# Filling the key and value buffers on ScalarE and adding the gathered rows in the transfer

## What is computed

```python
def _edge_attention(xn, edge_index, ef, ew, Wq, bq, Wk, bk, Wv, bv, We, be, Wo, bo):
    q = (xn @ Wq + bq).reshape(n, H, DH)          # H = 8 heads of DH = 32
    k = (xn @ Wk + bk).reshape(n, H, DH)
    v = (xn @ Wv + bv).reshape(n, H, DH)
    ep = ef @ We + be                             # the edge part, 32 numbers for all heads
    scores = jnp.einsum('ehd,ehd->eh', q[dst], k[src] + ep[:, None, :]) * scale
    scores = scores * ew[:, None]
    m = jax.ops.segment_max(scores, dst, num_segments=n)
    ex = jnp.exp(scores - m[dst])
    s = jax.ops.segment_sum(ex, dst, num_segments=n)
    attn = ex / s[dst]
    out = jax.ops.segment_sum(attn[:, :, None] * v[src], dst, num_segments=n)
    return out.reshape(n, D) @ Wo + bo
```

## Time and profile before

| | us |
|---|---|
| median of 3 runs | 2762.05 |
| lowest and highest run | 2761.53, 2766.91 |
| span of the profiled execution, first to last instruction | 2736.8 |
| attention loop in it (first gather's issue to VectorE's last operation) | 1401 to 2680 |

### The profile page before, as it was taken

One profiled execution on the slowest core, in us unless ns is written; L12 is line 12 of the kernel. 1 busy time (PEld: TensorE's weight loads), 2 busy tenths in 40 slices (PEclk: granted clock), 3 DMA queues, 4 the chain that ended last, 5 costly groups with the idle time before them and its releaser, 6 DMA issues. The chain is left out here.

```text
span 2736.8 us, 41806 instructions
## 1 busy us (share of the span) xinstructions
PE 2107.6 (77%) x9647; PEld 1611.0 (59%) x9647; DVE 2183.1 (80%) x3415; ACT 1524.3 (56%) x4291; POOL 1618.3 (59%) x1808
## 2 busy tenths in 40 slices
PE   3999999999999999679815666666566666656666
PEld 2787878777777777533314455455455545545555
DVE  6888888888888888645546878878888788878793
ACT  5787888788877887433223444444444444444443
POOL 5666666666666666342246666666666666666642
PEclk8999999999999999889957788878878878887787
DMA  6232222222222222769856666666666666666651
GB/s 203 72 84 81 83 83 83 83 82 84 83 83 81 84 82 84 167 165 253 234 181 168 168 173 175 173 165 173 177 169 175 169 172 176 167 175 170 173 141 45
DMA packets 157414, 379.08 MB, mean 139 GB/s; under 512 B 47810, under 2 KB 63298, under 8 KB 157186
## 3 DMA queue, kind: packets, MB, share of 16 engines
q0 software_dynamic: 100544, 309.00, 40.6%
q1 hardware_dynamic: 44946, 68.53, 8.7%
q10 hardware_dynamic: 11904, 1.34, 0.4%
HBM read 353.36 MB, written 37.07 MB: 143 GB/s over the span
## 5 line engine op out<-in xcount | busy, mean ns | idle before, releaser
L1358 POOL DMA_INDIRECT kv_e<-kv_rows,edge x752 | 716.9, 953 | 408.4 <-issue 223.4
L487 POOL DMA_INDIRECT feat<-in_x_rows,idx x664 | 677.1, 1020 | 236.2 <-issue 234.8
L523 ACT ACTIVATE vsh<-feat,rec_a 128x256 f32<-128x256 f32 x1980 | 806.8, 495 | 8.9 <-DMA feat<-in_x_rows,idx 4.8
L1541 PE MATMUL ps_sum<-kv_e,ident 128*128 128x264 f32 x1504 | 473.8, 477 | 376.9 <-issue 264.2
L1541 PEld LDWEIGHTS ps_sum<-kv_e,ident 128*128 128x128 f32 x1504 | 352.5, 240 | 481.8 <-issue 283.6
L571 PE MATMUL ps_a<-msg,hot 128*128 128x257 f32 x1312 | 409.4, 393 | 4.0 <-issue 4.0
L573 PE MATMUL ps_a<-msg,hot 128*128 128x256 f32 x1312 | 390.6, 379 | 0.1
L575 PE MATMUL ps_a<-msg,hot 128*128 128x192 f32 x1312 | 320.2, 325 | 0.0
L573 PEld LDWEIGHTS ps_a<-msg,hot 128*128 128x128 f32 x1312 | 248.6, 190 | 38.2 <-issue 1.9
L575 PEld LDWEIGHTS ps_a<-msg,hot 128*128 128x128 f32 x1312 | 248.8, 190 | 34.9
L571 PEld LDWEIGHTS ps_a<-msg,hot 128*128 128x128 f32 x1312 | 222.2, 189 | 66.3 <-issue 66.3
(11 more groups left out here) (419 smaller groups left out, 3182.2 us busy)
## 6 DMA issues: line engine op xcount, KB each, us to landing
ef<-in_ef_t SPq DMA_DIRECT2D x84, 256.0 KB
kv_e<-kv_rows,edge POOLq DMA_INDIRECT x752
rows_e<-rows SPq DMA_DIRECT2D x41, 272.0 KB
feat<-in_x_rows,idx POOLq DMA_INDIRECT x664
rows_e<-in_ef_t SPq DMA_DIRECT2D x1, 7446.0 KB, 26.6
kv_rows<-kv SPq DMA_DIRECT2D x20, 260.0 KB, 2.5
rows_e<-in_ef_t SPq DMA_DIRECT2D x1, 3706.0 KB
x<-x_rows SPq DMA_DIRECT2D x23, 128.0 KB
```

Source lines behind the costliest of these rows:

```text
L487: pool.indirect_dma_start(out=feat[:, u, c, 0, :, :].rearrange("p a b -> p (a b)"), out_offset=None, in_=g.x_rows, in_offset=bass.Indirect ...
L523: ins = act.activation(vsh[:, u % TURN, c, j, :, :], feat[:, u % TURN, c, 0, :, :], ACT.Copy, scale=rec_a[:, u % 2, c, 1 + j:2 + j])
L1358: pool.indirect_dma_start(out=kv[:, u, s, :], out_offset=None, in_=g.kv_rows, in_offset=bass.IndirectOffsetOnAxis(ap=edge[:, u, s, DH + 1: ...
L1541: mm = pe.matmul(out, g.ident[:], kv[:, u, s, D:], start=(s == 0), stop=False, skip_group_check=True)
```

## The change

ScalarE prepares each buffer before its gathers: `clear` writes zeros into the value part (8 slots of 264) and `part` writes the edge part, repeated for the 8 heads, into the key part (two halves of 4 slots of 256). GpSimd waits for this, by the new semaphore `v_fill`, where it waited for `v_used`; ScalarE itself waits for `v_used` before `clear`. The gathers carry an addition: each row is added to what lies in the buffer. VectorE's `keys` is gone, and `scores` waits for the gathers itself. In ScalarE's step `part` moves ahead of `query`. The semaphore counts on VectorE change from six to five a step (left out below).

```diff
--- before.py
+++ after.py
...
@@ -1344,7 +1345,7 @@
 
                 k = t * RING + u
                 pool.wait_ge(v_edge[u], t * 16 + 16)
-                pool.wait_ge(v_used, k * 2 + 1)
+                pool.wait_ge(v_fill, k * 2 + 1)
                 pool.sem_inc(v_asked_pool, 1)
                 for s in range(SLOTS):
                     if s == SLOTS // 2:
@@ -1353,11 +1354,12 @@
                             pool.wait_ge(v_read, k + 1)
                             pool.sem_inc(v_asked_pool, 1)
                             edges((u + 1) % RING)
-                        pool.wait_ge(v_used, k * 2 + 2)
+                        pool.wait_ge(v_fill, k * 2 + 2)
                         pool.sem_inc(v_asked_pool, 1)
                     pool.indirect_dma_start(
                         out=kv[:, u, s, :], out_offset=None, in_=g.kv_rows,
                         in_offset=bass.IndirectOffsetOnAxis(ap=edge[:, u, s, DH + 1:DH + 2], axis=0),
+                        compute_op=ALU.add,
                     ).then_inc(v_kv[u], 16)
 
             with pool.Fori(0, whole) as t:
@@ -1397,13 +1399,21 @@
             def query(u, w):
 
                 act.activation(ps_q[:, u, 1, :], g.q[:, bass.ds(w, 1), :].rearrange("p a d -> p (a d)"), ACT.Copy)
-                act.activation(beyond[:, u, :], count1[:], ACT.Relu, bias=now[:, u, 1:2])
+                act.activation(beyond[:, u, :], count1[:], ACT.Relu, bias=now[:, u, 1:2]).then_inc(v_query, 1)
+
+            def clear(u):
+
+                act.activation(kv[:, u, :, D:], zero[:].rearrange("p (a b) -> p a b", a=1).broadcast_to(
+                    [P, SLOTS, HEADS * HEAD]), ACT.Copy)
 
             def part(u, landed):
 
                 act.wait_ge(v_edge[u], landed)
-                act.activation(ps_q[:, u, 0, :].rearrange("p (s d) -> p s d", s=SLOTS), edge_f[:, u, :, 0:DH],
-                               ACT.Copy).then_inc(v_query, 1)
+                for half in range(2):
+                    slots = slice(half * HALF, (half + 1) * HALF)
+                    own = edge_f[:, u, slots, 0:DH].rearrange("p s (a d) -> p s a d", a=1)
+                    act.activation(kv[:, u, slots, 0:D].rearrange("p s (h d) -> p s h d", h=HEADS),
+                                   own.broadcast_to([P, HALF, HEADS, DH]), ACT.Copy).then_inc(v_fill, 1)
 
             def old(u):
 
@@ -1433,12 +1443,16 @@
                 act.activation(weight, score[:, u, 0:SLOTS, :], ACT.Exp)
                 act.activation(fade[:, u, :], score[:, u, SLOTS, :], ACT.Exp).then_inc(v_fade, 1)
                 old((u + 1) % RING)
-                query((u + LEAD) % RING, before)
                 if ahead:
                     part((u + 2) % RING, (t + (u + 2) // RING) * 16 + 16)
+                query((u + LEAD) % RING, before)
                 act.wait_ge(v_kept, k + 1)
                 act.sem_inc(v_asked_act, 1)
                 keep(k, u - 1)
+                if ahead:
+                    act.wait_ge(v_used, k * 2 + 2 * RING)
+                    act.sem_inc(v_asked_act, 1)
+                    clear((u + LEAD) % RING)
                 return w
 
             def gelu(f):
@@ -1484,8 +1498,12 @@
             act.wait_ge(v_const, 10)
             act.sem_inc(v_asked_act, 1)
             old(0)
+            act.wait_ge(v_edge[0], 16)
+            act.sem_inc(v_asked_act, 1)
             for u in range(2):
+                clear(u)
                 part(u, 16)
+            clear(2)
             with act.Fori(0, whole) as t:
                 w = None
                 for u, piece in enumerate((normed_out, attention_out, deviations, None)):
@@ -1736,35 +1754,28 @@
             dve.tensor_scalar(g.w_2[:], g.w_2[:], g.beta_s[:], None, ALU.mult).then_inc(v_const, 1)
             dve.tensor_scalar(g.b_2[:], g.b_2[:], g.beta_s[:], None, ALU.mult).then_inc(v_const, 1)
 
-            def keys(k, t, u):
-
-                dve.wait_ge(v_kv[u], (t + 1) * (16 * SLOTS))
-                rows = kv[:, u, :, 0:D].rearrange("p s (h d) -> p s h d", h=HEADS)
-                part = ps_q[:, u, 0, :].rearrange("p (s a d) -> p s a d", s=SLOTS, a=1)
-                dve.wait_ge(v_query, k + 1)
-                dve.tensor_tensor(rows, rows, part.broadcast_to([P, SLOTS, HEADS, DH]), ALU.add).then_inc(v_own, 1)
-
-            def scores(k, u):
+            def scores(k, t, u):
 
                 rows = kv[:, u, :, 0:D]
                 s = score[:, u, 0:SLOTS, :]
-                dve.wait_ge(v_own, k * 6 + 1)
+                dve.wait_ge(v_query, k + 1)
+                dve.wait_ge(v_kv[u], (t + 1) * (16 * SLOTS))
                 dve.tensor_tensor(rows, rows, ps_q[:, u, 1:2, :].broadcast_to([P, SLOTS, D]),
                                   ALU.mult).then_inc(v_own, 1)
...
@@ -1826,20 +1837,16 @@
                 dve.memset(spare[:], 0.0)
                 dve.bn_aggr(mv[:, 1, :], stats[:, 1, :]).then_inc(w_dve, 1)
 
-            keys(0, 0, 0)
             with dve.Fori(0, whole) as t:
                 for u, piece in enumerate((divide, None, spread, norms)):
                     k = t * RING + u
-                    scores(k, u)
-                    keys(k + 1, t + (u + 1) // RING, (u + 1) % RING)
+                    scores(k, t, u)
                     values(k, u)
                     if piece:
                         piece(t)
             for u in range(TAIL):
                 k = whole * RING + u
-                scores(k, u)
-                if u + 1 < TAIL:
-                    keys(k + 1, whole, u + 1)
+                scores(k, whole, u)
                 values(k, u)
             out = done_window(dve, whole)
             dve.wait_ge(w_act, whole * 3 + 1)
```

More of the change, by code:

```diff
@@ L1242, in stage_attend @@
         v_query = ctx.enter_context(nc.semaphore("v_query"))
+        v_fill = ctx.enter_context(nc.semaphore("v_fill"))
         v_fade = ctx.enter_context(nc.semaphore("v_fade"))
@@ L1737, in _ @@
             dve.tensor_scalar(g.b_2[:], g.b_2[:], g.beta_s[:], None, ALU.mult).then_inc(v_const, 1)
-            def keys(k, t, u):
-                dve.wait_ge(v_kv[u], (t + 1) * (16 * SLOTS))
-                rows = kv[:, u, :, 0:D].rearrange("p s (h d) -> p s h d", h=HEADS)
-                part = ps_q[:, u, 0, :].rearrange("p (s a d) -> p s a d", s=SLOTS, a=1)
-                dve.wait_ge(v_query, k + 1)
-                dve.tensor_tensor(rows, rows, part.broadcast_to([P, SLOTS, HEADS, DH]), ALU.add).then_inc(v_own, 1)
-            def scores(k, u):
+            def scores(k, t, u):
                 rows = kv[:, u, :, 0:D]
                 s = score[:, u, 0:SLOTS, :]
-                dve.wait_ge(v_own, k * 6 + 1)
+                dve.wait_ge(v_query, k + 1)
+                dve.wait_ge(v_kv[u], (t + 1) * (16 * SLOTS))
                 dve.tensor_tensor(rows, rows, ps_q[:, u, 1:2, :].broadcast_to([P, SLOTS, D]),
                                   ALU.mult).then_inc(v_own, 1)
-                dve.wait_ge(v_own, k * 6 + 2)
+                dve.wait_ge(v_own, k * 5 + 1)
                 dve.tensor_reduce(s, rows.rearrange("p s (h d) -> p s h d", h=HEADS), AX.X, ALU.add).then_inc(v_own, 1)
-                dve.wait_ge(v_own, k * 6 + 3)
+                dve.wait_ge(v_own, k * 5 + 2)
                 dve.tensor_tensor(s, s, edge_f[:, u, :, DH:DH + 1].broadcast_to([P, SLOTS, HEADS]),
@@ L1759, in scores @@
                 dve.wait_ge(v_old, k + 1)
-                dve.wait_ge(v_own, k * 6 + 4)
+                dve.wait_ge(v_own, k * 5 + 3)
                 dve.scalar_tensor_tensor(s, beyond[:, u, :].rearrange("p (s a) -> p s a", a=1).broadcast_to([P, SLOTS, HEADS]),
@@ L1763, in scores @@
                 dve.sem_inc(v_read, 1)
-                dve.wait_ge(v_own, k * 6 + 5)
+                dve.wait_ge(v_own, k * 5 + 4)
                 every = score[:, u, :, :]
                 dve.tensor_reduce(top[:, u, :], every.rearrange("p s h -> p h s"), AX.X, ALU.max).then_inc(v_own, 1)
-                dve.wait_ge(v_own, k * 6 + 6)
+                dve.wait_ge(v_own, k * 5 + 5)
                 dve.tensor_tensor(every, every, top[:, u:u + 1, :].broadcast_to([P, SLOTS + 1, HEADS]),
```

## The result

| | before | after |
|---|---|---|
| median of 4 runs, us | 2761.79 | 2987.69 |
| lowest and highest | 2759.22, 2766.91 | 2985.78, 2989.58 |
| ratio, 95% interval | | 1.082 [1.080, 1.084] |
| span of the profiled execution | 2736.8 | 2985.8 |

The change costs 8.2%, 226 us. The forecast was 1.3% (2797); its range ended at 2990. What follows shows the size of the error in one number, the length of a step.

A forecast was written before the change was run, and what follows sets the result against it. VectorE led GpSimd by only 0.1 us, so GpSimd became the bound: 11.3 + 1.9 (waits) + 0.5 (issues) = 13.7 us a step against 13.33, +35 us over 94 steps, 2797 us (1.3% slower); range 2690 to 2990.

The forecast's parts named there:

- The issue's price: GpSimd's issue of each adding gather: 60 ns more than a plain one, 0.5 us a step.
- the ceiling from L908: Upper limit for the added issue cost, from the costliest issue of any kind (1347 ns): 0.39 us an issue, 3.2 a step.
- The third rival: GpSimd's issue grows by 0.2 to 0.3 us each, giving 2865 to 2912 us; chance 0.13.
- The waits: Waiting in the attention loop, mostly VectorE's for TensorE's semaphores, taken as unchanged: 1.9 us a step, bounds 0.9 and 2.5.
- The transfer: The gathers' DMA, reading each row from memory and from the buffer: no cost taken in the steady state; least certain choice.
- the second rival: Transfers become the bound: at the doubled price 16.3 us a step, 3041 us, halfway 2900; chance 0.24.
- The shortened lead: GpSimd's gather prefetch loses its lead of three steps, since ScalarE's fill after v_arg of step k releases step k+2.
- the closed loop of two steps: From exponentials through fill, gathers, landing and scores: sum 21.4 us, 10.7 a step, 0.6 under GpSimd's 11.3.
- a stall now reaches GpSimd: VectorE or ScalarE stalls reach the gathers; VectorE's slack of 1.9 us a step absorbs short ones, not 8.2 and 8.9 us.
- VectorE off the path: Without its 2.28 us addition VectorE's pace falls from 11.41 to 9.4 us a step, under GpSimd's 11.3.
- the exponentials exposed: Between scores and values nothing runs on VectorE any more, so ScalarE's exponentials show: 0.27 us a step.
- The offset: Median of the runs above the profiled span, left as it is: 25.25 us, from 2771.8 to 2797.

The follow-up runs named there:

- short_rows: The changed kernel with adding gathers of half-length rows (260 numbers in place of 520): 16.0 us a step; its total, 3396 us in one run, can't be compared.
- half_add: The changed kernel with only every second of the eight gathers adding, the other four overwriting: 2775.44 us, 13.8 us a step.
- three_of_eight: The changed kernel with three of eight gathers adding, five overwriting: 2697.96 us, ratio 1.069 to a kernel before that took 2523.84 us there.
- plain64: The changed kernel with plain, overwriting gathers of 64 rows in place of 128: 3057 us in a single run, 16.8 us a step.
- light_fill: The changed kernel with plain gathers and ScalarE's fills cut to 8 and 4 elements a partition, all waits kept: 3034.74 us, ratio 1.097.
- plain_after: The changed kernel with gathers that overwrite in place of adding, everything else of the change kept: 2983.56 us, ratio 1.081.

## Why the prediction was wrong in its size

1. **The issue's price, the step that failed.** I took 60 ns for the addition, "near the indirect forms", with 0.39 us as the ceiling from L908. Measured: 583 ns, 4.7 us a step in place of 0.5. Even the ceiling was too low, for it came from another kind of issue, and nothing in the trace tied the two. With 583 ns, and without the waits of the next point, the sum gives 11.3 + 4.7 = 16.0, which is the result; with them it would be 17.9. The third rival had the mechanism ("GpSimd's issue grows"), at 0.2 to 0.3 us. The Trainium skill, Perfetto Trace Analysis, section "DMA Instruction — SWDGE (GPSIMD)", says that the profiled interval of such an issue ends when the last descriptor is generated, not when data has moved. The half-length rows agree: 1536 ns either way. That the same issue, alone in the kernel before, gives 2988.44 us shows that this step is enough for the whole loss.
2. **The waits, 1.9 us "as they are".** The second step that failed. They went to nothing: no TensorE signal of 229 in the loop was over 1 us late, where 145 of 253 had been. VectorE's slack, 16.0 - 9.4 = 6.6 us a step, would have swallowed most of them, but had none to swallow. The forecast took the lateness as a constant of the kernel, and it changes with the pace and, as the 2524 us show, from one comparison to the next. (Of the 1.92 us a step, 1.5 were waits on "remote".)
3. **The transfer, taken at no cost.** Its time nearly doubled, as the second rival said: 0.97 x 16.0 = 15.5 us a step of DMA time against 0.63 x 13.33 = 8.4. The estimate was 16.3. It is the second bound, 0.5 us behind GpSimd, and not the one that sets the time, as short_rows shows (share 0.58, the same step). The last rows landed 4.2 us after the last issue (2910.40 to 2914.62), 3.0 were forecast. The Trainium skill, Collectives: The Full Stack, section "The bandwidth ceiling: the fold count and why AG ≠ RS ≠ AR", gives the reducing step of a ring of cores, which reads two sources for each chunk, about half the rate of a copying one. The trace agrees for this gather on one core: 143 / 0.97 = 147 GB/s while busy against 172 / 0.63 = 273. Whether the second read or the doubled number of packets does it, no run tells apart.
4. **The shortened lead.** That the closed loop of two steps does not bind by itself was right down to 13.2 us a step: in half_add and three_of_eight GpSimd never waits over 0.3 us for the fill. Its 10.7 us are not tested. That "a stall now reaches GpSimd" was right too, and mis-sized: with plain gathers 4.6 us a step, not 1.9. In the changed kernel there is no such stall.
5. **Right as put:** VectorE off the path (8.9 us of work a step), the exponentials exposed by 0.29 us, ScalarE at 592.6 / 62.5 = 9.5 us a step with 1.06 and 1.96 us for the fills (1.03 and 1.94 forecast), VectorE's end 12.9 us after the last issue (12 forecast), and 11.3 us a step as GpSimd's bound for plain gathers.
6. **The offset.** I left the median 25.25 us above the profiled span. After, it is 1.9 us (2987.69 against 2985.8). The profiled execution of before was a quick one.

In numbers: the step's error of 2.3 us x 94 = 216, less 23 from the offset, gives 193; between 2797 and 2988 lie 191.

## What to carry to other kernels

An operand that makes a gather add is paid three times, in the issuing engine's time, in the transfer and in the buffer that must be filled ahead, and the issue is the one that the trace of before cannot price: run one such instruction before the design rests on it. A wait for late signals that a trace shows is not a constant to be added to the next bound: here it vanished when GpSimd became slower. And where taking work off the busiest engine changes nothing, look for late signals, and try a mixture: where signals were late, three adding gathers of eight beat both none and all, by 1.1% and 9%.

## What the runs showed of the hardware

- An adding indirect gather of 128 rows holds GpSimd for 1536 ns (953 to 960 plain), of 64 rows 1407 (907 plain); halving the bytes of a row made no difference to the adding one (1536).
- TensorE's signals can reach the waiting engine 17.8 us after the matmul's recorded end, while TensorE is idle. In one comparison of seven none was late in the loops traced, and the kernel before took 8.6% less there (2524 against 2762). What makes them late stays open: they were late with a DMA share of 0.27 (plain64) and with ScalarE's fills cut to nothing (light_fill).
- Late signals come in bunches (each within 1 us of the one ahead), and the bunches stand mostly where GpSimd has stopped issuing: in light_fill 28 of 33 bunches came 3.0 to 3.5 us after the end of GpSimd's last issue, and in the kernel before 38 of 71 came more than 1.5 us after it, though GpSimd stood that long in only 7% of the time. A rival that no run tests follows: plain issues 1.26 us apart hold TensorE's signals back, and a pause or a longer issue lets them through. But GpSimd also stops because the signals are late, so the order in time alone does not show it.
- How much of this reaches the end is a matter of pace. Where signals were late, the kernels with 13.1 us or more of issues a step had no wait on "remote" over 0.3 us, and those traced with 12.6 or less had up to 195 us of them on one line in 1000 (light_fill). That an engine with less to do made the kernel slower (plain_after against half_add, 208 us) goes with it. Why a gap so small brings the waits back is not explained.
